# Decay exponents in gated cross attention: the key side carried by the same product as the peaks

## The chip, the cores and the metric

The kernel runs on one core of a Trainium2 chip. The metric is the device time of one execution in microseconds; three executions of the kernel before took 3082.6, 3076.7 and 3079.26 us, with a median of 3079.26 us.

## What is computed

Two layers act on `x` of 32 sequences with 512 tokens and 512 features. The first is a gated cross attention of 8 heads of 64 in the manner of an mLSTM: its queries are the normalized rows of `x`, its keys and values are the raw `ctx` rows, and each score is multiplied by a decay factor. The second is a feed-forward layer of 8 experts, in which each expert takes the 2048 tokens with its highest probabilities. The change lies in the first layer, whose core is:

```python
log_f = log_sigmoid(fg)                       # gates: a linear map of q and ctx, 8 heads
cs = cumsum(log_f, axis=-1)
log_D = where(tril, cs[..., :, None] - cs[..., None, :], -inf) + ig[..., None, :]
max_log_D = max(log_D, axis=-1, keepdims=True)
D = exp(log_D - max_log_D)
C = (q @ k.T / sqrt(64)) * D
h = (C / (maximum(abs(C.sum(-1)), exp(-max_log_D)) + 1e-6)) @ v
x = x + tanh(g) * (normalize_per_head(h) * out_w)
...
x = x + tanh(g2) * experts(layernorm(x))
```

## The kernel before, in words

**Stages.** An attention stage goes through the 32 sequences one by one and takes the first third of the time; it leaves the new `x`, its normalized rows and the expert probabilities in memory. The rest is the experts, which the change doesn't touch.

**Attention as a pipeline.** Each of the five engines has a hand-written program with a loop `for i in range(NB + 2)`; one pass is called a round. In round i an engine works on several sequences at once: `b1 = i - 1` has its gates computed and its keys and queries turned, `b2 = i - 2` has its scores weighted and its values summed, `b3 = i - 3` gets its heads normalized and added to `x`, `b4` and `b5` have the new rows normalized. Each engine runs its instructions strictly in the written order and waits on semaphores; nothing reorders them. A sequence is cut into four tiles of 128 tokens: within a tile the scores are computed in full, and between tiles a state `S` is carried.

**Decay exponents.** Within a tile the exponent of a key s and a query t is rise[s] minus a peak over the keys up to t. `gate_runs` on VectorE writes `rise` (L1052), 32 rows for each of the four tiles (`QD`), the first 16 of which hold the 8 heads twice: once for the rounded part and once for the remainder that the rounding leaves, since the matrix product takes rounded numbers (fp32r). GpSimd's `split_climb` (L383) makes the two parts, `climb_low` and `climb`. `gate_peaks` on VectorE (L1057) writes `peaks` in the same manner. TensorE's `decays(b, p)` (L741) gathers the exponents of a pair of heads p in the tile `EX`: first four products lay the causal mask (L749), then two products of 64x512 add the key side, with `climb` as weights and `pick` as the columns that choose heads (L754), then four products of 64x256 subtract the peaks, with `sel` as the constant weights that choose a head (L760). The two halves of the array's rows work beside each other. ScalarE takes the exponential of `EX` into `C` (L457), and VectorE multiplies it with the scores `QK` (L1017).

**Order around the change.** TensorE's round holds `decays(b2, 1)`, `decays(b2, 2)`, `decays(b2, 3)` and at its end `decays(b1, 0)`. Ahead of `decays(b2, 3)` stands `shift_gates(b1)` (L706), which moves the input gates to the rows of the forget gates for `rise`. Which PSUM bank a transpose, a state or a gate product fills is laid down in the list of `iteration_fills`, whose last number is a bank: 0 and 1 are `T`, 2 and 3 are the two halves of `QK`; for a half of `QK` a fill waits until VectorE has weighted the scores in it. GpSimd's round is: `centred_values(b1)` (`vc`), wait for VectorE's reciprocal roots (`nn`, L960), weigh the heads of b3 (L233, four tiles), `split_climb(b1)`, weigh the columns (L240, four tiles), add tile 0 to `x` (L246), the weighted values `uv` of b1 (L379), add tiles 1 to 3, which ends with the signal `x2`. VectorE waits for `x2` of a round in the next one, ahead of the row statistics of b4 (`st`, L903), and everything behind them on VectorE waits with it, among it the roots that lead to `nn`. SyncE issues all loads and stores of the stage on one queue.

## Time and profile before

| | before |
|---|---|
| median of three runs | 3079.26 us |
| the profiled execution | 3074.24 us |
| its span, first to last instruction | 3072.5 us |
| TensorE busy over the span | 2964.4 us (96%) |
| VectorE, ScalarE, GpSimd busy | 1832.6, 1138.2, 1057.8 us |
| mean granted clock of TensorE | 0.986 |

All rows are from that one profiled execution. A time stands in microseconds from the span's start; a row that joins several instructions of one line gives the start of the first and the time to the end of the last. An idle time in brackets names what ended it. Rows of 100 to 1000 us belong to the attention stage.

### The profile page before, as it was taken

How to read it: one execution, taken by the hardware profiler on the slowest of the kernel's cores; microseconds unless marked ns; L12 is line 12 of the kernel's file. 1: busy time of each engine (PE TensorE's matmuls, PEld its weight loads, DVE VectorE, ACT ScalarE, POOL GpSimd, SP SyncE). 2: the span in 40 equal slices, each digit the busy share in tenths (PEclk: the TensorE clock that was granted, in tenths of full speed). 3: DMA queues.
4: the chain of work that ended last, by engine and by line, in shares of the span. 5: the costliest groups of instructions: out<-in, count | busy, mean ns of one | idle time of the engine just before them, and what ended most of it. 6: DMA issues, size and time to landing. Idle time of an engine off the chain costs nothing.

```text
span 3072.5 us, 60746 instructions
## 1 busy us (share of the span) xinstructions
PE 2964.4 (96%) x24708; PEld 2398.2 (78%) x24708; DVE 1832.6 (60%) x5124; ACT 1138.2 (37%) x2025; POOL 1057.8 (34%) x1028
## 2 busy tenths in 40 slices
PE   6999999999997599999999999999999999999998
PEld 5888888888886477777777777787787777778886
DVE  6999998999998645354454444445435444444322
ACT  5778787877886311121121121122112112112110
POOL 4767687777766211111112111121112111121111
PEclk9999999999998799999999999999999999999999
DMA  3243434434342422231242131232123214222121
GB/s 129 84 166 113 167 135 144 158 121 167 130 149 104 137 42 35 37 99 31 44 100 47 37 79 34 37 95 62 31 37 88 45 31 110 37 49 58 35 37 23
DMA packets 140062, 250.68 MB, mean 82 GB/s; under 512 B 31457, under 2 KB 31457, under 8 KB 139785
## 3 DMA queue, kind: packets, MB, share of 16 engines
q1 hardware_dynamic: 105784, 170.80, 16.5%
q0 software_dynamic: 28672, 67.65, 12.5%
q10 hardware_dynamic: 5328, 8.36, 0.9%
q8 instruction: 196, 3.21, 0.4%
q14 instruction: 82, 0.66, 0.1%
HBM read 137.23 MB, written 101.19 MB: 78 GB/s over the span
## 4 chain that ended last, share of the span: by engine, by line
PE 63%; DMA 2%; DVE 1%; issue 0%; ACT 0%; POOL 0%; ACTq 0%; DVEq 0%; POOLq 0%
PE DN L1710 31%; PE UP L1684 29%; PE TT L1657 2%; DMA w_raw<-in_L_ffn_W_down 2%; DVE c_hit L1380 0%; DVE down_lo L1246 0%; PE c_bank L1373 0%; ACT z L1629 0%; PE c_bank L1357 0%; DVE c_hit L1401 0%; DVE c_within L1396 0%; ACT down_hi L1240 0%; POOL out_x L1604 0%; DVE mid_lo L1742 0%; DVE c_gained L1433 0%
## 5 line engine op out<-in xcount | busy, mean ns | idle before, releaser
L1604 POOL DMA_INDIRECT out_x<-y,slots x128 | 202.0, 1578 | 1640.5 <-DVE y L1764 1640.5
L1710 PE MATMUL DN<-down_hi,mid_hi 128*128 128x512 f32 x1408 | 579.2, 411 | 0.0
L1629 ACT ACTIVATE z<-UP,bup 128x512 f32<-128x512 f32 (+1 forms) x352 | 240.8, 686 | 853.8 <-PE UP L1684 836.9
L1684 PE MATMUL UP<-xT_hi,up_hi 128*128 128x512 f32 (+1 forms) x1408 | 553.1, 393 | 1.9 <-DVE xT_lo L1721 0.9
L1684 PE MATMUL UP<-xT_hi,up_lo 128*128 128x512 f32 (+1 forms) x1408 | 554.8, 394 | 0.0
L1684 PE MATMUL UP<-xT_lo,up_hi 128*128 128x512 f32 (+1 forms) x1408 | 551.3, 392 | 0.0
L1710 PE MATMUL DN<-down_hi,mid_lo 128*128 128x512 f32 x1280 | 505.1, 395 | 0.0
L1710 PE MATMUL DN<-down_lo,mid_hi 128*128 128x512 f32 x1280 | 504.9, 394 | 0.0
L1740 DVE CAST mid_hi<-z 128x512 fp32r<-128x512 f32 (+1 forms) x352 | 151.1, 429 | 484.3 <-ACT z L1629 484.3
L1613 ACT ACTIVATE xT_hi<-TT 128x512 fp32r<-128x512 f32 x126 | 75.1, 597 | 702.9 <-PE TT L1657 682.9
L1684 PEld LDWEIGHTS UP<-xT_hi,up_hi 128*128 128x128 f32 (+1 forms) x1408 | 259.8, 185 | 68.5 <-ACT z L1629 4.5
L1684 PEld LDWEIGHTS UP<-xT_lo,up_hi 128*128 128x128 f32 (+1 forms) x1408 | 259.3, 184 | 66.7
L1684 PEld LDWEIGHTS UP<-xT_hi,up_lo 128*128 128x128 f32 (+1 forms) x1408 | 259.6, 184 | 65.3
L1710 PEld LDWEIGHTS DN<-down_hi,mid_hi 128*128 128x128 f32 x1408 | 265.6, 189 | 51.9
L1710 PEld LDWEIGHTS DN<-down_hi,mid_lo 128*128 128x128 f32 x1280 | 240.0, 187 | 58.7
L1762 DVE TENSOR_TENSOR y<-DN,bdn 128x512 f32<-128x512 f32 x128 | 88.5, 692 | 330.5 <-PE DN L1710 326.1
L1710 PEld LDWEIGHTS DN<-down_lo,mid_hi 128*128 128x128 f32 x1280 | 241.1, 188 | 46.0
L1742 DVE TENSOR_TENSOR mid_lo<-z,mid_hi 128x512 fp32r<-128x512 f32 (+1 forms) x352 | 244.3, 694 | 12.1
L233 POOL TENSOR_TENSOR nsb<-nsb,rr 128x512 f32<-128x512 f32 x125 | 127.0, 1048 | 225.2 <-DVE nn L960 225.2
L1017 DVE SCALAR_TENSOR_TENSOR C<-QK,C 128x512 f32<-128x512 f32 x256 | 164.7, 685 | 8.5 <-PE QK L738 6.5
L903 DVE BATCH_NORM_STATS2 st<-xs 128x6 f32<-128x512 f32 x248 | 152.9, 679 | 14.4 <-DMA xs<-in_x 14.0
L738 PE MATMUL QK<-qT,kT 64*128 64x128 f32 x2048 | 147.3, 283 | 14.7 <-DVE S L1035 13.6
(263 smaller groups left out, 5005.3 us busy)
## 6 DMA issues: line engine op xcount, KB each, us to landing
xs<-in_x SPq DMA_DIRECT2D x32, 1024.0 KB, 8.3
kraw<-in_ctx SPq DMA_DIRECT2D x32, 1024.0 KB, 5.7
out_x<-xs SPq DMA_DIRECT2D x32, 1024.0 KB, 12.7
rows_scratch<-xfb SPq DMA_DIRECT2D x32, 1024.0 KB, 10.8
w_raw<-in_L_ffn_W_down SPq DMA_DIRECT2D x40, 512.0 KB, 4.4
w_raw<-in_L_ffn_W_up SPq DMA_DIRECT2D x16, 682.5 KB, 4.1
mid_hi<-mid_hi ACTq DMA_DIRECT2D x32, 86.0 KB
mid_lo<-mid_hi ACTq DMA_DIRECT2D x32, 84.0 KB
```

Of the source, the lines that this page charges most:

```text
L233: ins = eng.tensor_tensor(n, n, spread(scale[:, j, :], 2, DH), ALU.mult)
L738: mm = pe.matmul(QK[:, par, jj], kT[r, b % 2, p, jj], qT[r, b % 2, p, jj], start=True, stop=True)
L903: dve.bn_stats(st[:, which, j, :], src[:, j, :]).then_inc(s["dchain"], 1)
L1017: dve.scalar_tensor_tensor(out=c, in0=QK[:, par, :], scalar=DH ** -0.5, in1=c, op0=ALU.mult, op1=ALU.mult)\
L1604: pool.indirect_dma_start(out_rows, bass.IndirectOffsetOnAxis(ap=slots[:, m:m + 1], axis=0), y[:, t, :], None, compute_op=ALU.add).then_in ...
L1613: act.activation(xT[0][:, c, :], turned(n, c)[:, :], ACT.Copy).then_inc(s["thi"], 1)
L1629: act.activation(z[0:r, k % 2, :], UP[k % 3][0:r, :], ACT.Silu, bias=bup[0:r, e // 2, f:f + 1]).then_inc(s["z"], 1)
L1684: mm = pe.matmul(UP[k % 3][0:r, :], weights.up[wa][:, c, f * P:f * P + r], xT[xa][:, c, :], start=first, stop=(c == CH - 1 and wa == 1))
L1710: mm = pe.matmul(DN[m % 2][:, :], lhs, rhs, start=first, stop=(f == FCH - 1 and lhs is parts[-1][0]))
L1740: dve.tensor_copy(mid[0][0:r, f, :], z[0:r, k % 2, :]).then_inc(s["hi"], 1)
L1742: dve.tensor_tensor(mid[1][0:r, f, :], z[0:r, k % 2, :], mid[0][0:r, f, :].bitcast(FP32), ALU.subtract)\
L1762: dve.tensor_tensor(y[:, t, :], DN[m % 2][:, :], bdn[:, e % 2, :], ALU.add).then_inc(s["yp"], 1)
```

## The change

The `climb` and `pick` products leave `decays`. Instead the four products that subtract the peaks carry the key side too. Their weights are no longer the constant `sel` but a tile `climbs`, which holds for each head the parts of `rise` in rows that were empty before, masked to that head by `ofhead`, and -1 in the rows of the peaks; against the `rise` rows stand ones in `peaks`, laid once among the constants. For this the 16 rows of `rise` of each tile must move by 16 partitions: SyncE copies them to a tile `lift` with four small copies for each sequence (`lift_rise`), and `split_climb` works on `lift`. `spread_climb` on GpSimd writes `climbs`, first for the heads of pair 0, later for the other six. `climbs` has one buffer where `climb` had two. The weighted values of b1 now come ahead of all four row sums, and the first column product ahead of `split_climb`. `shift` gets bank 2 in place of 1, and `scores(b2, 3)` waits for it to be taken.

```diff
-        sel = sb("sel", [P, HEADS, P], FP32R); selP = sb("selP", [P, HEADS, DH], FP32R)
+        climbs = sb("climbs", [P, HEADS, P], FP32R); ofhead = sb("ofhead", [P, HEADS]); selP = sb("selP", [P, HEADS, DH], FP32R)
...
-        climb = sb("climb", [P, 2, P], FP32R); climb_low = sb("climb_low", [P, P], FP32R)
-        pick = sb("pick", [P, PAIRS, 2, 2], FP32R)
+        climb = sb("climb", [P, P], FP32R); climb_low = sb("climb_low", [P, P], FP32R)
+        lift = sb("lift", [P, P]); lift_lows = sb("lift_lows", [P, TILES])
...
-                    ("qw", b2, 2, "dve", 1), ("scores", b2, 2, None, None), ("shift", b1, 0, "dve", 1), ("qw", b2, 3, "dve", 1),
+                    ("qw", b2, 2, "dve", 1), ("scores", b2, 2, None, None), ("shift", b1, 0, "dve", 2), ("qw", b2, 3, "dve", 1), ("scores", b2, 3, None, None),
...
+                def lift_rise(b):
+
+                    wait_taken(sp, "shift", b, 0)
+                    if b:
+                        sp.wait_ge(s["rp"], b)
+                    for j in range(TILES):
+                        at = QD * j
+                        sp.dma_start(lift[at + 2 * HEADS:at + QD, :], rise[at:at + 2 * HEADS, :]).then_inc(s["lifted"], 16)
...
                     store_probabilities(i - 7)
+                    if live(i - 1):
+                        lift_rise(i - 1)
...
-                        if row % QD < 2 * HEADS:
-                            step(pool.affine_select(out=heads[:, :], in_=heads[:, :], compare_op=ALU.not_equal, fill=1.0,
+                        for one in (heads, ofhead) if row % QD < 2 * HEADS else (ofhead,):
+                            step(pool.affine_select(out=one[:, :], in_=one[:, :], compare_op=ALU.not_equal, fill=1.0,
...
-                    step(pool.tensor_scalar(sel[:, :, :], spread(heads[:, :], 2, P), -1.0, None, ALU.mult))
...
+                    for n in range(2):
+                        step(pool.tensor_copy(peaks[:, n, :], C[:, 5, :]))
...
-                    wait_taken(pool, "shift", b, 0)
-                    if b >= 2:
-                        pool.wait_ge(s["ee"], 2 * PAIRS * (b - 1))
-                    step(pool.tensor_scalar(climb_low[:, :], rise[:, :], lows[:, 0:1], None, ALU.mult))
-                    pool.tensor_tensor(climb[:, b % 2, :], rise[:, :], climb_low[:, :].bitcast(FP32), ALU.subtract).then_inc(s["rp"], 1)
+                    pool.wait_ge(s["lifted"], 16 * TILES * (b + 1))
+                    step(pool.tensor_scalar(climb_low[:, :], lift[:, :], lift_lows[:, 0:1], None, ALU.mult))
+                    pool.tensor_tensor(climb[:, :], lift[:, :], climb_low[:, :].bitcast(FP32), ALU.subtract).then_inc(s["rp"], 1)
                     pool.wait_ge(s["rp"], b + 1)
+                    if b:
+                        pool.wait_ge(s["ee"], 2 * PAIRS * b)
+                    spread_climb(b, 0, 2)
+
+                def spread_climb(b, first, end):
+
+                    heads_of = climbs[:, first:end, :]
+                    pool.tensor_tensor(heads_of, spread(climb[:, :].bitcast(FP32), 1, end - first), spread(ofhead[:, first:end], 2, P), ALU.mult)\
+                        .then_inc(s["cl"], 1)
+                    pool.wait_ge(s["cl"], 2 * b + (1 if first == 0 else 2))
...
-                    if p == 0:
-                        pe.wait_ge(s["rp"], b + 1)
-                    for a, r in ((0, top), (1, end)):
-                        ones_of = pick[r, p, :, :].rearrange("k a j -> k (a j)")
-                        pe.matmul(EX[:, a, :], climb[r, b % 2, :], spread(ones_of, 2, P), start=False, stop=False, skip_group_check=True)
+                    if p < 2:
+                        pe.wait_ge(s["cl"], 2 * b + p + 1)
...
-                            mm = pe.matmul(EX[:, a, par * 2 * P:(par + 1) * 2 * P], sel[r, 2 * p + par, :], peaks[r, b % 2, half],
+                            mm = pe.matmul(EX[:, a, par * 2 * P:(par + 1) * 2 * P], climbs[r, 2 * p + par, :], peaks[r, b % 2, half],
...
                     if b >= 1:
-                        dve.wait_ge(s["rp"], b)
+                        dve.wait_ge(s["lifted"], 16 * TILES * b)
...
-                        rows = slice(QD * j, QD * j + QD)
+                        rows = slice(QD * j, QD * j + 2 * HEADS)
```

How this stands on the engines is shown at three places; each row is a line of the kernel, an operation, its tiles and the count of equal neighbours. The first is GpSimd's round from the heads of b3 (`nsb`) to the row sums, before and then after:

```order
L233 TENSOR_TENSOR nsb<-nsb,rr 128x8x64 x4
L388 TENSOR_SCALAR climb_low<-rise,lows 128x128
L389 TENSOR_TENSOR climb<-rise,climb_low 128x128
L240 TENSOR_TENSOR nsb<-nsb,Wo 128x8x64 x4
L246 TENSOR_TENSOR xs<-xs,nsb 128x512
L379 TENSOR_TENSOR uv<-vc,tm 128x520 x3
L246 TENSOR_TENSOR xs<-xs,nsb 128x512 x3
```

```order
L233 TENSOR_TENSOR nsb<-nsb,rr 128x8x64 x4
L240 TENSOR_TENSOR nsb<-nsb,Wo 128x8x64
L404 TENSOR_SCALAR climb_low<-lift,lift_lows 128x128
L405 TENSOR_TENSOR climb<-lift,climb_low 128x128
L414 TENSOR_TENSOR climbs<-climb,ofhead 128x256
L240 TENSOR_TENSOR nsb<-nsb,Wo 128x8x64 x3
L397 TENSOR_TENSOR uv<-vc,tm 128x520 x3
L414 TENSOR_TENSOR climbs<-climb,ofhead 128x768
L246 TENSOR_TENSOR xs<-xs,nsb 128x512 x4
```

Two products with `climbs` have come in ahead of the row sums, one column product has moved ahead of `climb_low`, and the weighted values stand ahead of all row sums. The second place is TensorE from `shift` to the scores of pair 3:

```order
L706 MATMUL T<-gsum,shift 128x128
L749 MATMUL EX<-maskneg,identb 64x512
L749 MATMUL EX<-maskswap,identb 64x512 x2
L749 MATMUL EX<-maskneg,identb 64x512
L754 MATMUL EX<-pick,climb 128x512 x2
L760 MATMUL EX<-peaks,sel 128x256 x4
L768 MATMUL T<-inner,selP 128x384
L713 MATMUL T<-ends,later 128x8
L714 MATMUL T<-unseen,ident 128x4
L738 MATMUL QK<-qT,kT 128x128 x8
```

```order
L734 MATMUL QK<-gsum,shift 128x128
L777 MATMUL EX<-maskneg,identb 64x512
L777 MATMUL EX<-maskswap,identb 64x512 x2
L777 MATMUL EX<-maskneg,identb 64x512
L785 MATMUL EX<-peaks,climbs 128x256 x4
L793 MATMUL T<-inner,selP 128x384
L741 MATMUL T<-ends,later 128x8
L742 MATMUL T<-unseen,ident 128x4
L766 MATMUL QK<-qT,kT 128x128 x8
```

The pair of products with `climb` is gone, and `shift` fills a half of `QK`. The third place is SyncE's round:

```order
L290 DMA kraw<-in_ctx 128x4x512 [waits a_vc,a_tfull]
L294 DMA xs<-in_x 128x4x512 [waits a_xf2,a_xst0]
L259 DMA rows_scratch<-xfb 128x4x512 [waits a_xf2]
L254 DMA out_x<-xs 128x4x512 [waits a_x2]
L264 DMA rows_scratch<-sm_all 128x4x8 [waits a_smx]
L284 DMA lift<-rise 16x128 [waits a_rp,a_td]
L284 DMA lift<-rise 16x128 x3
```

The five large transfers of a round stand as before, and the four copies to `lift` have come in behind them.

## Rows read from the trace of the kernel before

**Rows 1.** Stretches, `rise` to `rise`: length, busy by engine (instructions), PEclk, DMA share, GB/s

```profile
85.11:113.20 28.09, 26.59 (x444) 22.16 (x442) 26.45 (x72) 19.10 (x38) 20.05 (x21) 1.00 0.22 77
...
469.59:498.74 29.15, 28.79 (x491) 24.55 (x487) 27.20 (x78) 23.61 (x47) 21.82 (x23) 1.00 0.44 147
529.05:559.65 30.60, 30.37 (x491) 25.84 (x487) 27.30 (x78) 23.31 (x47) 20.49 (x22) 0.94 0.41 140
...
sum 830.48, PE 811.47 PEld 689.52 DVE 763.37 ACT 659.61 POOL 611.51; mean PE 28.98 PEld 24.63 DVE 27.26 ACT 23.56 POOL 21.84
```

**Rows 2.** Waits from 100 to 1000 us: total, times, longest

```profile
PE QK L738 <- DVE S L1035: 12.9, 26, 0.9
DVE st L903 <- DMA xs<-in_x: 10.1, 13, 2.2
DVE qw L1026 <- PE T L768: 9.5, 24, 1.0
DVE rise L1052 <- PE T L706: 5.6, 13, 1.4
```

**Rows 3.** TensorE in order of time: start, length, line, operation, count, idle before

```profile
485.42 1.16 PE L738 MATMUL QK<-qT,kT 64*128 64x128 f32 x16 [0.36 <-DVE S L1035]
...
498.15 0.49 PE L706 MATMUL T<-gsum,shift 128*128 128x128 f32 x2
...
498.91 0.48 PE L754 MATMUL EX<-pick,climb 64*128 64x512 f32 x2
499.23 0.40 PE L760 MATMUL EX<-peaks,sel 64*128 64x256 f32 x4
...
504.62 0.48 PE L754 MATMUL EX<-pick,climb 64*128 64x512 f32 x2
...
512.69 0.48 PE L754 MATMUL EX<-pick,climb 64*128 64x512 f32 x2
```

**Rows 4.** VectorE in order of time, the same stretch

```profile
487.83 2.46 DVE L903 BATCH_NORM_STATS2 st<-xs 128x6 f32<-128x512 f32 x4
...
496.59 0.17 DVE L960 SCALAR_TENSOR_TENSOR nn<-mv,rr 128x8 f32<-128x8 f32 x1
...
498.74 0.29 DVE L1052 TENSOR_TENSOR rise<-T,cs 128x128 f32<-128x128 f32 x1 [0.30 <-PE T L706]
```

**Rows 5.** GpSimd in order of time, from the heads to the row sums

```profile
496.90 4.05 POOL L233 TENSOR_TENSOR nsb<-nsb,rr 128x512 f32<-128x512 f32 x4 [6.74 <-DVE nn L960]
501.05 0.61 POOL L388 TENSOR_SCALAR climb_low<-rise,lows 128x128 fp32r<-128x128 f32 x1
501.74 0.46 POOL L389 TENSOR_TENSOR climb<-rise,climb_low 128x128 fp32r<-128x128 f32 x1
502.28 4.61 POOL L240 TENSOR_TENSOR nsb<-nsb,Wo 128x512 f32<-128x512 f32 x4
...
508.14 3.08 POOL L379 TENSOR_TENSOR uv<-vc,tm 128x520 f32<-128x520 f32 x3
511.29 3.46 POOL L246 TENSOR_TENSOR xs<-xs,nsb 128x512 f32<-128x512 f32 x3
```

**Rows 6.** Store of `sm_all` on SyncE: shortest, median, longest issue (ns) and landing

```profile
L264 SPq DMA_DIRECT2D rows_scratch<-sm_all x32: 360/1904/2438, 191.1 to 1007.6; - x32
...
DMA to landing us min/median/max: 1.8/12.5/13.3
```

**Rows 7.** Transfers of the whole run: line's tiles, KB, us from issue to landing

```profile
tanh_g<-in_g_ffn ACTq DMA_DIRECT2D x1, 0.5 KB, 2.6
```

**Rows 8.** The stretch from 497 to 498 us, columns as in the first group

```profile
497.00:498.00 1.00, 1.00 (x26) 0.93 (x22) 0.96 (x2) 0.94 (x5) 1.00 (x2) 1.00 0.09 26
```

**Rows 9.** Prologue in order of time, GpSimd's constants

```profile
9.21 0.61 POOL L318 CAST selP<-C 128x512 fp32r<-128x512 f32 x1
9.91 2.79 POOL L319 TENSOR_SCALAR sel<-C 128x1024 fp32r<-128x1024 f32 x1
```

**Rows 10.** TensorE's first product with `peaks`

```profile
33.71 0.80 PE L760 MATMUL EX<-peaks,sel 64*128 64x256 f32 x4 [2.13 <-DVE peaks L1071]
```

More of the change, by code:

```diff
@@ L303, in _ @@
                 step = Chain(pool, s["pchain"])
+                step(pool.memset(lift[:, :], -1.0))
                 for n in range(2):
@@ L325, in constants @@
-                    step(pool.tensor_tensor(lows[:, 0:2], lows[:, 0:2], lows[:, 2:4], ALU.add))
-                    step(pool.tensor_tensor(lows[:, 0:1], lows[:, 0:1], lows[:, 1:2], ALU.add))
+                    for rows, first in ((lows, HEADS), (lift_lows, 3 * HEADS)):
+                        step(pool.memset(rows[:, :], 1.0))
+                        step(pool.affine_select(out=rows[:, :], in_=rows[:, :], compare_op=ALU.is_ge, fill=0.0,
+                                                base=-first, pattern=[[-QD, TILES]], channel_multiplier=1))
+                        step(pool.affine_select(out=rows[:, :], in_=rows[:, :], compare_op=ALU.is_ge, fill=0.0,
+                                                base=first + HEADS - 1, pattern=[[QD, TILES]], channel_multiplier=-1))
+                        step(pool.tensor_tensor(rows[:, 0:2], rows[:, 0:2], rows[:, 2:4], ALU.add))
+                        step(pool.tensor_tensor(rows[:, 0:1], rows[:, 0:1], rows[:, 1:2], ALU.add))
@@ new lines, in constants @@
+                    ones_of = C[:, 5, :].rearrange("p (j t) -> p j t", j=TILES)
+                    step(pool.memset(ones_of, 1.0))
+                    step(pool.affine_select(out=ones_of, in_=ones_of, compare_op=ALU.is_ge, fill=0.0,
+                                            base=-2 * HEADS, pattern=[[-QD, TILES], [0, P]], channel_multiplier=1))
+                    step(pool.affine_select(out=ones_of, in_=ones_of, compare_op=ALU.is_ge, fill=0.0,
+                                            base=QD - 1, pattern=[[QD, TILES], [0, P]], channel_multiplier=-1))
@@ L334, in constants @@
                                             base=QD - 1, pattern=[[QD, TILES]], channel_multiplier=-1))
-                    step(pool.tensor_tensor(wt[:, 0:2], own[:, 0:2], own[:, 2:4], ALU.add))
-                    step(pool.tensor_tensor(pick[:, :, :, :].rearrange("k p a j -> k (p a) j"), spread(heads[:, :], 2, 2),
-                                            spread(wt[:, 0:2], 1, HEADS), ALU.mult))
                     step(pool.memset(unseen[:, :], 0.0))
@@ L400, in _ @@
                         weigh_heads(step, pool, b3, slice(0, TILES))
+                    if live(b3):
+                        weigh_columns(step, pool, b3, slice(0, 1))
                     if live(b1):
@@ L403, in _ @@
                     if live(b3):
-                        weigh_columns(step, pool, b3, slice(0, TILES))
+                        weigh_columns(step, pool, b3, slice(1, TILES))
+                    if live(b1):
+                        weigh_v(b1)
+                        spread_climb(b1, 2, HEADS)
+                    if live(b3):
                         for j in range(TILES):
-                            if j == 1 and live(b1):
-                                weigh_v(b1)
                             ins = add_rows(pool, b3, j)
@@ L885, in _ @@
                 ins.then_inc(s["clear"], 1)
-                for t in (gW[:, :, :], peaks[:, :, :].bitcast(FP32), inner[:, :, :].bitcast(FP32)):
+                for t in (gW[:, :, :], inner[:, :, :].bitcast(FP32)):
                     step(dve.memset(t, 0.0))
```

10 lines of the change are left out of this document (2 added, 8 removed).

## The prediction
> **What bounds the kernel now.** I read first the table of stretches, cut at the decay chain's `rise` of each sequence, because the diff touches the attention stage alone. A sequence takes 29.15 us where nothing disturbs it, and 28 sequences take 830.48 us, 29.66 each [rows 1]. TensorE is busy for 28.79 of the 29.15 us, VectorE for 27.20, GpSimd for 21.82 [rows 1]. This looks like a TensorE bound, but the list of waits says that it is nearly two bounds: TensorE waits for VectorE's `S` (12.9 us in 26 waits) and VectorE waits for TensorE's `qw` fill (9.5 us, 24) and for its `shift` product (5.6 us, 13) [rows 2]. So the two hand the lead to each other: TensorE leads from the scores of pair 1 (it waited 0.36 us there) to `shift`, VectorE from `rise` (it waited 0.30 us) to `S` [rows 3, 4].
>
> There is a third ring, and the change puts its new work into it. VectorE ends `nn` at 496.59 + 0.17 = 496.76; GpSimd starts on the heads at 496.90 and ends the row sums (`x2`) at 511.29 + 3.46 = 514.75 [rows 4, 5]. VectorE needs `x2` for the row statistics of the next round, which stand at 487.83 in this one, so at 516.98 a period later; from there to its next `nn` it works 496.76 - 487.83 = 8.93 us without a wait of note [rows 4]. The ring is thus 0.14 + 17.85 + 8.93, with about 0.1 us for the signal of `x2` (an estimate between the handovers seen in these rows, 0.04 to 0.15): 27.02 us. It fits into 29.15 with 2.1 us to spare. GpSimd is idle long enough, but its idle time stands ahead of the heads, where it waits for `nn`, not inside this run.
>
> **TensorE: two products fewer for each pair.** The 64x512 products with `climb` start at 498.91 and those with `peaks` at 499.23 [rows 3]; the two run beside each other on the two halves of the array, so a pair gives up 0.32 us, a sequence 4 x 0.32 = 1.28 us, 32 sequences 41 us. The product that now carries both sides keeps its shape (four of 64x256), so it costs nothing more. If TensorE alone set the time, 41 us would come back. It doesn't: in the path that alternates, TensorE leads over one pair only (pair 2) and VectorE's wait for `qw` ends earlier by the 0.32 us of another (pair 3). VectorE's wait of 0.30 us for `shift` goes, and 0.32 of the 0.40 us (9.5 in 24 [rows 2]) for `qw`; then it is full: 29.15 - 0.62 = 28.5 us for a sequence is the floor of these two engines. The rest of the 1.28 us becomes waiting of TensorE.
>
> **GpSimd: the heads are spread.** New are a product of 128x256 (pair 0) ahead of most of the column weights and one of 128x768 behind the weighted values, both ahead of the row sums, so both inside the third ring. The trace has no such instruction. The nearest are products of two inputs, one of them repeated: 128x520 at 3.08 us for three [rows 5], 1.03 us each and 1.06 with the 0.03 us by which neighbours overlap, and the `climb` difference of 128x128 at 0.46 us [rows 5]. A line through 0.46 and 1.06 gives 0.27 us + 1.53 ns a column: 0.66 and 1.43 us, 2.09 us together. From below, a cast of 128x512 takes 0.61 us with one input [rows 9], two such sizes 1.2 us; from above, the old `sel`, a 128x1024 product with a constant, took 2.79 us [rows 9], with a second start about 3.0. I take 2.09, whose rows have the operation and the operands. The extra steps cost their handovers: one more between the first and the other three column weights (0.10 us), one behind each spread (0.08 us each, as between 501.05 + 0.61 and 501.74 [rows 5]), and the overlap of 0.03 us of a row sum with the weighted values: 0.28 us. The run becomes 17.85 + 2.09 + 0.28 = 20.22 us and the ring 0.14 + 20.22 + 0.10 + 8.93 = **29.4 us**. That is above the two-engine floor of 28.5 and above the undisturbed 29.15.
>
> The page "GPSIMD Engine Reference" of the Trainium skill, section "Elementwise — side-by-side cycle accounting", speaks against the move: a product of two tensors costs GpSimd some 2.2 ns a column (4497 ns for 2048 columns), about twice VectorE's price. The rows here show 2.0 with a repeated operand; by the page's figure the spreads would be 2.25 us (an estimate) and the ring 29.55.
>
> **Spreading pair 0 first, weighted values earlier.** Counted from `nn`, GpSimd now ends pair 0 at 7.4 us (0.14 + 4.05 heads + 0.10 + 1.19 first column, a quarter of 4.61 with its overlap + 0.09 + 0.61 + 0.08 + 0.46 + 0.08 + 0.66). TensorE reached that product 504.62 - 498.15 = 6.47 us behind the start of `shift` [rows 3] and now 0.32 us less; with `shift` about 0.7 us behind `nn`, since it now lies in a score bank and must wait until VectorE has weighted those scores, that is 6.9 us. So it waits some 0.5 us, which its 1.28 us pay. Its next product of this kind comes 512.69 - 504.62 = 8.07 us later [rows 3], less 0.32: 15.2; heads 2 to 7 are ready at 15.6. Another 0.4 us of waiting, also covered. The weighted values begin at 11.0 us behind `nn`, 0.3 earlier than the 508.14 of before [rows 5], and TensorE's use of them keeps its distance. Behind the row sums stand SyncE's store of `x` and GpSimd's next values; the store leaves 2.3 us later, and the slot that it empties is loaded again only a round after that.
>
> **SyncE: four small copies.** `rise` ends some 2.0 us behind `nn` (the 0.30 us wait for `shift` is gone). SyncE wakes and issues four copies of 8 KB, at 0.36 us or a little more each [rows 6], the last at about 3.3. From issue to landing the trace has 1.8 us at the least for a store on this queue when nothing stands ahead of it [rows 6], and 2.6 us for a small load [rows 7]. The copies land between 5.1 and 5.9; GpSimd comes for them at 5.5. So they cost between 0 and 0.4 us in the ring, and I take 0, for the store is on the same queue. The queue is empty then: the engines' share falls to 0.09 at 497 us, a microsecond ahead of `rise` [rows 8]. If the cover failed, each 0.1 us would cost 2.8 us of the time. Queued behind the waiting SyncE are only the loads of the next round, issued 14 us later.
>
> **What disturbs now and then.** The mean lies 0.51 us above 29.15. Part is the wait for `xs` (10.1 us in 13 [rows 2]); VectorE comes for it 0.9 us later after the change, so most of this goes. Part is two sequences in which the granted clock averaged 0.94 of full speed (one of them 30.60 us [rows 1]) and a few stalls of TensorE; about 0.7 us of each is now covered by the ring. I leave 2.5 us in all.
>
> **Ends.** GpSimd's constants grow: sixteen more selections, `lift_lows`, `ones_of` and two copies of 128x512 into `peaks` (0.61 us each by the cast [rows 9]), less the 2.79 us of `sel`: about 6 us, an estimate. VectorE's first gates hardly feel it, but pair 0 of the first sequence waited for `peaks` until 33.71 [rows 10] and will wait for GpSimd until about 35: 1.2 us. The two first rounds, without row sums, win 0.7 us each; the fourth goes from 28.09 us [rows 1] to 29.4, a loss of 1.3.
>
> **Sum.** 27 full rounds at 29.4 in place of 29.66: -7.3 us; a last short round -0.6; disturbances +2.5; ends 1.2 - 1.4 + 1.3 = +1.1. Together -4 us. The profiled execution took 3074.24 us, 1.7 more than its span of 3072.5 and 5.0 less than the median of the three runs, 3079.26; the difference is carried to the median: **3075 us**.
>
> **Rivals.** (a) *The third ring doesn't decide*: the spreads cost near their lower end, 1.2 us. Then the ring is 28.5, level with the two engines' floor; 27 x (29.66 - 28.6) = 28 us, less the disturbances and ends: 3053. For it: GpSimd's price a column is read from shapes at most 520 wide. Against: the cast is an operation with one input, and GpSimd's products of two run at one price here, four of them in 4.05 to 4.61 us [rows 5]. (b) *Slower, by the landing of the copies*: issue at 0.45 us each and landing at 2.6 us put `lift` at 6.1 behind `nn`, 0.6 us into the ring: 30.0 us, +17 us, 3092. It decides from 5.5 us on, and only there. For it: the small load took 2.6 us; against: the idle queue's 1.8. The Trainium skill's page "DMA: Bandwidth & Descriptors", section "Anatomy of one DMA — SWDGE (gpsimd) path", gives about 2.0 us fixed, which would put the landing at 5.3 (an estimate), inside the cover. (c) *Slower, by the spreads at `sel`'s price*, 3.0 us: ring 30.3, 3100. (d) *The change doesn't save what it says*: the `climb` products were hidden beside weight loads and TensorE's 28.79 us stay near 28.5; with the two new waits of 0.9 us a sequence takes 29.5 and the time is 3081. Against: the next product's start moves with them in all four pairs.
>
> **Chances.** Forecast 0.52 (3066 to 3085), (a) 0.17, (b) 0.18, (c) 0.06, (d) 0.07. About 0.2%, 6 us, is what a measurement of this kernel can tell from no change. Of the forecast's share a third falls under 3073, so faster has 0.17 + 0.17 = 0.34; slower 0.15 + 0.06 + 0.03 + 0.02 = 0.26; the same 0.40. The range of 8 in 10 takes in the cheap spreads and the late copies: 3053 to 3094.
>
> **What would show it.** In the profile of the changed kernel: VectorE waits for GpSimd's `xs` at the second row statistics, about 1 us in each round (step "ring"); TensorE's idle time grows by about 1.5 us a sequence, mostly at the products with `climbs`; the two spreads take 0.66 and 1.43 us; GpSimd waits for `lift` less than 0.2 us; `rise` to `rise` is 29.4 us and steadier. If VectorE never waits for `x2`, (a) is right; if GpSimd's wait ahead of `climb_low` is over 0.4 us, (b).

## The result, and the profile after

Slower: 3144.27 us (median of 4 runs, 3135.57 to 3147.56) against 3078.5 us for the kernel before on the same chip; the ratio is 1.0212 with a 95% interval of 1.0197 to 1.0227, some 66 us. The prediction said 3075 us and a range up to 3094. The profiled execution took 3144.76 us, its span 3143.0 us, the mean granted clock was 0.973 of full speed (0.986 before).

Stretches of the kernel after from `rise` to `rise`, as in [rows 1] (length; busy PE, PEld, DVE, ACT, POOL; PEclk, DMA share, GB/s). The sum is over the 27 rounds from 117 to 976 us:

```profile
532.43:562.97 30.54, 28.35 (x481) 23.79 (x483) 28.45 (x77) 23.59 (x47) 23.91 (x25) 1.00 0.41 141
562.97:594.36 31.39, 28.35 (x481) 23.79 (x483) 29.31 (x78) 23.74 (x47) 23.89 (x25) 1.00 0.41 138
...
626.40:659.31 32.91, 31.18 (x481) 26.28 (x483) 29.31 (x77) 23.44 (x47) 23.89 (x25) 0.90 0.38 131
...
sum 858.97, PE 802.67 PEld 674.31 DVE 772.94 ACT 636.26 POOL 645.29; mean PE 29.73 PEld 24.97 DVE 28.63 ACT 23.57 POOL 23.90
```

A mean round is 31.81 us in place of 29.66 [rows 1]. From the first `rise` to the last the kernel takes 61.7 us more (976.2 against 914.5), out of 70.5 us by which the spans of the two profiles differ; nearly all of the rest lies behind the last `rise`, and its cause is open. There are three kinds of round: undisturbed ones of 30.5 us (the first row), ones at full clock that are longer all the same (the second), and ones in which TensorE's granted clock averages 0.95 or less, mostly 0.90 or 0.95 (the third). The prediction had 29.4 for all.

GpSimd in the undisturbed round, in order of time (start, length, line, operation, count, idle before), answering to [rows 5]:

```profile
531.01 4.05 POOL L233 TENSOR_TENSOR nsb<-nsb,rr 128x512 f32<-128x512 f32 x4 [5.75 <-DVE nn L985]
...
537.69 0.61 POOL L414 TENSOR_TENSOR climbs<-climb,ofhead 128x256 fp32r<-128x256 f32 x1
...
545.12 1.47 POOL L414 TENSOR_TENSOR climbs<-climb,ofhead 128x768 fp32r<-128x768 f32 x1
546.67 4.61 POOL L246 TENSOR_TENSOR xs<-xs,nsb 128x512 f32<-128x512 f32 x4
...
551.75 4.05 POOL L387 TENSOR_TENSOR vc<-kraw,hs 128x512 f32<-128x512 f32 x4
```

VectorE in the same round, answering to [rows 4]:

```profile
551.32 2.47 DVE L928 BATCH_NORM_STATS2 st<-xs 128x6 f32<-128x512 f32 x4 [0.59 <-POOL xs L246]
...
554.24 0.60 DVE L969 TENSOR_TENSOR top<-nsb,tm 128x32 f32<-128x32 f32 x1
554.88 0.97 DVE L970 SCALAR_TENSOR_TENSOR top<-nsb,top 128x32 f32<-128x32 f32 x1
555.88 0.18 DVE L971 TENSOR_SCALAR top<-top 128x32 f32<-128x32 f32 x1
...
561.24 0.17 DVE L985 SCALAR_TENSOR_TENSOR nn<-mv,rr 128x8 f32<-128x8 f32 x1
```

Here the ring of the prediction can be read off. GpSimd works from 531.01 to 551.28, VectorE takes `x2` 0.04 us later (it had waited 0.59 us for it) and ends `nn` at 561.41: 0.14 + 20.27 + 0.04 + 10.09 = 30.54 us, the length of the round. It closes as foretold, and in 27 of 28 rounds: there VectorE takes `x2` within 0.1 us of its end. But VectorE's part is 10.09 us and not 8.93. The two instructions on `top` (L969, L970) take 0.60 and 0.97 us, and 0.21 each in rounds where GpSimd is idle beside them: 1.15 us. They stand beside GpSimd's `vc`, which follows the row sums at once. In the kernel before, `vc` (GpSimd, until 519.27) was over when VectorE came to them:

```profile
515.22 4.05 POOL L369 TENSOR_TENSOR vc<-kraw,hs 128x512 f32<-128x512 f32 x4
```

```profile
519.90 0.21 DVE L944 TENSOR_TENSOR top<-nsb,tm 128x32 f32<-128x32 f32 x1
520.15 0.21 DVE L945 SCALAR_TENSOR_TENSOR top<-nsb,top 128x32 f32<-128x32 f32 x1
```

Below, "company" means GpSimd at work beside such small instructions of VectorE.

Waits from 100 to 1000 us (total, times, longest), answering to [rows 2]:

```profile
POOL climb_low L404 <- DMA lift<-rise: 24.2, 17, 1.9
...
PE QK L734 <- DVE C L1042: 20.6, 16, 2.1
PE EX L785 <- POOL climbs L414: 13.6, 25, 1.3
...
DVE st L928 <- POOL xs L246: 12.6, 17, 1.0
```

GpSimd waits for the copies in 17 rounds, 1.4 us in the mean; a wait for `xs` from memory no longer stands in the list. The copies themselves, SyncE's line L284 (issue in ns at the least, median, most; landing in us):

```profile
L284 SPq DMA_DIRECT2D lift<-rise x112: 512/589/1578, 117.5 to 978.3; - x112
...
DMA to landing us min/median/max: 1.6/1.7/3.5
```

### The profile page after: what moved, and what is told of

It reads as the page before. It is cut to its first block, busy times and chain, and to the rows that moved or that the text cites. A ratio compares the mean times of both kernels' runs of the same rounds, so it can differ in the third digit from the quotient of the medians.

```text
span 3143.0 us, 60592 instructions
## 1 busy us (share of the span) xinstructions
PE 2982.9 (95%) x24452; PEld 2404.1 (76%) x24452; DVE 1867.8 (59%) x5123; ACT 1137.7 (36%) x2025; POOL 1129.9 (36%) x1117
## 4 chain that ended last, share of the span: by engine, by line
PE 61%; DMA 2%; DVE 2%; issue 0%; ACT 0%; POOL 0%; ACTq 0%; DVEq 0%; POOLq 0%
PE DN L1735 31%; PE UP L1709 28%; DMA w_raw<-in_L_ffn_W_down 2%; PE TT L1682 2%; DVE c_hit L1405 0%; DVE down_lo L1271 0%; PE c_bank L1398 0%; ACT z L1654 0%; PE c_bank L1382 0%; DVE c_hit L1426 0%; DVE mid_lo L1767 0%; DVE c_within L1421 0%; ACT down_hi L1265 0%; POOL out_x L1629 0%; DVE mid_hi L1765 0%
## 5 line engine op out<-in xcount | busy, mean ns | idle before, releaser
L766 PE MATMUL QK<-qT,kT 64*128 64x128 f32 x2048 | 161.1, 302 | 8.8 <-DVE S L1060 8.0
L928 DVE BATCH_NORM_STATS2 st<-xs 128x6 f32<-128x512 f32 x248 | 153.0, 679 | 18.4 <-POOL xs L246 13.6
```

Of the source, the lines that this page charges most:

```text
L766: mm = pe.matmul(QK[:, par, jj], kT[r, b % 2, p, jj], qT[r, b % 2, p, jj], start=True, stop=True)
L928: dve.bn_stats(st[:, which, j, :], src[:, j, :]).then_inc(s["dchain"], 1)
```

## The experiments

Ratios are to the kernel before on the same chip, with their 95% interval. "Mean round" is over the same 27 rounds of the profile.

### The spreads alone, in the kernel before

**e3**: GpSimd makes both spreads into a tile that nobody reads; `sel` is kept once for each head, to make room.

```diff
+        step(pool.tensor_tensor(unread[:, 0:n, :], spread(climb[:, b % 2, :].bitcast(FP32), 1, n), spread(ofhead[:, 0:n], 2, P), ALU.mult))
```

> The kernel before with GpSimd's new work alone: two products of 128x256 and 128x768 into a tile that nobody reads, at the places where the change spreads the heads, and nothing else of the change (no copies by SyncE, climb products kept; to make room in memory the constant sel is held once for each head and repeated by its address pattern). Theory A: the ring becomes 0.14 + 20.1 + 0.05 + 10.1 = 30.4 us, so a round takes 30.4 in place of 29.7 and the time is 3095 to 3110; VectorE's two long instructions go from 0.21 to 0.6 and 0.97 us. If the ring doesn't decide, the time stays within 6 us of before.

Measured: 3100.39 us, 1.007 (1.0048 to 1.0092), rounds of 30.4, mean 30.50. With TensorE's work as before, 2.1 us on GpSimd cost 22 us. The number is the one expected, but by luck, for the ring stays open. In the round shown, GpSimd ends `x2` at 495.87 + 3.46 = 499.33 and VectorE comes for it at 499.85 without having waited; this slack of some 0.5 us stands in nearly every round. What grew is VectorE's own path. `sm_all` lasts 1.24 us (over 0.9 in 25 of 28 rounds) and the second `top` 0.90, beside GpSimd's `vc` here too; the kernel before had 0.19 and 0.21. That is 1.7 us more for a round that became 1.2 longer; VectorE's waits for TensorE took up the rest.

```profile
480.65:511.03 30.38, 28.88 (x483) 24.26 (x483) 28.88 (x78) 23.71 (x47) 23.88 (x25) 1.00 0.42 141
```

```profile
495.87 3.46 POOL L246 TENSOR_TENSOR xs<-xs,nsb 128x512 f32<-128x512 f32 x3
```

```profile
488.73 1.24 DVE L936 TENSOR_TENSOR sm_all<-ex,sx 128x32 f32<-128x32 f32 x1
...
499.85 2.46 DVE L910 BATCH_NORM_STATS2 st<-xs 128x6 f32<-128x512 f32 x4
...
503.01 0.90 DVE L952 SCALAR_TENSOR_TENSOR top<-nsb,top 128x32 f32<-128x32 f32 x1
```

`sm_all` in the kernel before:

```profile
506.93 0.19 DVE L929 TENSOR_TENSOR sm_all<-ex,sx 128x32 f32<-128x32 f32 x1
```

**e10**: e3 without the climb's two products for each pair (the exponents lack the climb).

```diff
-                        pe.matmul(EX[:, a, :], climb[r, b % 2, :], spread(ones_of, 2, P), start=False, stop=False, skip_group_check=True)
```

> The kernel before with GpSimd's two spreads (as in e3, whose rounds were 30.4 us at clock 1.00 and which took 3100 us), and now also without the climb's two products in each pair (so the exponents lack the climb): TensorE's load is that of the changed kernel, with no copies, no new wait of TensorE, and shift in its old bank. Theory clock: a lighter TensorE under a ring of 30.4 us waits about 2 us in each round, is granted the lower clock in some of them as the changed kernel without copies is (mean round 31.4 us, clock 0.974), and the kernel takes 3115 to 3130 us, slower by some 20 us although it does less. Rival ring alone: the rounds stay at 30.4 us whatever TensorE does, 3095 to 3103 us, and the clock dips of the changed kernel are due to its new waits.

Measured: 3106.85 us, 1.0103 (1.0081 to 1.0126); 21 of 27 rounds at clock 1.00 (26 in e3), mean round 30.75. Less work for TensorE won nothing and brought five more rounds at a lower clock; by time the two intervals overlap, so a loss is likely and not shown.

### VectorE's small instructions beside GpSimd

**e4, e1**: the variances (L969 to L974) ahead of the wait for `x2`, in the kernel before (e4) and after (e1).

```diff
+                    if live(b3):
+                        head_variances(b3)
                     if live(b4):
                         wait_x2(dve, b4)
...
-                    if live(b3):
-                        head_variances(b3)
```

> The kernel before with the same edit as the first of these runs (head variances ahead of the wait for x2). In the kernel before that wait is over long before, so theory A expects no more than 6 us either way, 3072 to 3085; if it moves by more, the order on VectorE matters in itself and the first run doesn't show the ring alone.

> The changed kernel with one edit on VectorE: the five small instructions of the head variances stand ahead of the wait for x2 instead of behind the row statistics. Theory A (the ring nn, GpSimd's run, x2, VectorE's run back to nn decides every round): the run back shrinks from 10.1 us to about 7.5, since 2.6 us of it (1.2 us of work, 1.2 to 1.4 us of two of its instructions standing while GpSimd works) leave it; a round falls from 31.8 us to 29.0 to 29.6, the time from 3144 to 3065 to 3090, and the granted clock in the attention stage rises, as TensorE waits less. Theory B (the low granted clock is a cause of its own that comes with fewer TensorE columns): the rounds stay at 31 us or more and the time at 3125 or more. The two long instructions should still be long (0.6 and 0.9 us) if GpSimd's row sums stand beside them, short (0.21) otherwise.

Measured: e4 3123.72 us, 1.0154 (1.0128 to 1.0179), steady rounds of 30.81; e1 3154.78 us, 1.025 (1.0229 to 1.0271). e4 missed its expectation and e1 its theory A; e1's time lies in the range of theory B, but the rows show another cause. In e4 VectorE now comes to the variances while `vc` runs (GpSimd's row first):

```profile
504.46 4.05 POOL L369 TENSOR_TENSOR vc<-kraw,hs 128x512 f32<-128x512 f32 x4
```

```profile
506.05 0.50 DVE L944 TENSOR_TENSOR top<-nsb,tm 128x32 f32<-128x32 f32 x1
506.59 0.97 DVE L945 SCALAR_TENSOR_TENSOR top<-nsb,top 128x32 f32<-128x32 f32 x1
507.59 0.96 DVE L946 TENSOR_SCALAR top<-top 128x32 f32<-128x32 f32 x1
```

In e1 the first three escape and the last two meet it; `vc` starts at 556.00:

```profile
555.69 0.21 DVE L970 SCALAR_TENSOR_TENSOR top<-nsb,top 128x32 f32<-128x32 f32 x1
555.93 0.18 DVE L971 TENSOR_SCALAR top<-top 128x32 f32<-128x32 f32 x1
556.15 0.94 DVE L972 SCALAR_TENSOR_TENSOR top<-top 128x32 f32<-128x32 f32 x1
557.12 0.97 DVE L974 SCALAR_TENSOR_TENSOR vv<-ssq,top 128x32 f32<-128x32 f32 x1
```

The same instructions last 0.2 us alone and up to 0.97 in these rows beside GpSimd, about one of GpSimd's pieces (4.05 us for four). In the attention stage of the kernels before and after, e1, e3, e4 and e10, 369 executions of the variances' instructions and of `sm_all` lasted over 0.4 us, and every one ended 0.03 to 0.05 us behind the end of an instruction of GpSimd: VectorE's instruction stands until that one has ended. This costs time even where no ring closes: VectorE comes for `x2` 5.0 us after it is ready in e4, 2.6 in e1 and 0.5 in e3 (medians). The Trainium skill's page "SBUF — State Buffer", section "SBUF: two separate sides", says that VectorE's instructions with two SBUF inputs and GpSimd's shut each other out of a shared pair of ports for a whole instruction. The rows agree for the two-input ones. The one-input L946 took 0.96 us too; it is a `TENSOR_SCALAR`, which the section "Who interferes with whom" of the same page of the Trainium skill says can run in a two-port mode that shares those ports, and no run here tells which mode it ran in.

**e7**: in the kernel after, the variances behind the new sequence's row statistics, when `vc` is over.

```diff
                         step(row_moments(xs[:, i % XBUF, :, :], 0))
+                    if live(b3):
+                        head_variances(b3)
                     row_variances(i)
```

> The changed kernel with the five small instructions of the heads' variances behind the row statistics of the new sequence instead of ahead of them, so that GpSimd's product vc, which begins once nn is used, has begun and mostly ended before they run. Theory ring with company: VectorE's run from x2 to nn falls from 10.1 towards 8.9 us where top is back at 0.21 us each, so rounds lose up to 1.1 us: 3105 to 3120 us. If top is still 0.6 and 0.97 us (GpSimd's rows products beside it): 3140 to 3150 us. Rival clock and late copies alone set the length: 3135 to 3150 us with top short.

Measured: 3151.37 us, 1.0231 (1.02 to 1.0263). `top` was back at 0.21 us, and nothing was won: VectorE now waited for the new `x`.

```profile
DVE st L928 <- DMA xs<-in_x: 29.9, 25, 2.7
```

**e11**: in the kernel after, ScalarE spreads heads 2 to 7 at the end of its round.

```diff
+                    for h in range(2, HEADS):
+                        ins = act.activation(climbs[:, h, :], climb[:, :].bitcast(FP32), ACT.Identity, scale=ofhead[:, h:h + 1])
```

> The changed kernel with the spread of heads 2 to 7 taken from GpSimd: ScalarE makes them at the end of its round, six instructions of 128x128 (its others of that shape take 0.28 to 0.39 us, so 1.8 us). GpSimd's stretch from nn to x2 falls by 1.47 to 18.9 us; if the ring closes at all it does so at about 28 us with top back at 0.21 us. Theory ring first: rounds are then set by TensorE and VectorE as before, 28.9 to 29.8 us, 3055 to 3090 us, and the clock dips get rarer since TensorE is busy for a larger part of a shorter round. Rival: copies and clock hold it, rounds of 30 us and more with clock under 0.97: 3095 to 3125 us.

Measured: 3136.53 us, 1.0183 (1.0134 to 1.0232), mean round 31.79, although GpSimd's ring no longer closed (VectorE comes for `x2` 1.3 us or more after it is ready). One round of 33.06 us, all at clock 1.00, was followed. Its rows on SyncE's queue, and VectorE's wait:

```profile
670.11 0.38 SPq L290 DMA_DIRECT2D kraw<-in_ctx  x1
671.05 0.38 SPq L294 DMA_DIRECT2D xs<-in_x  x1
```

```profile
681.02 2.47 DVE L938 BATCH_NORM_STATS2 st<-xs 128x6 f32<-128x512 f32 x4 [2.23 <-DMA xs<-in_x]
```

`rise` of that round stood at 654.06. The load of `kraw` goes out 16.05 us later, once the chunk states have freed its buffer; `x` follows 0.94 us behind it on the same queue, lands 9.97 us later, the statistics reach `nn` in 4.54 and the next `rise` comes in another 1.56: 33.06 us. That is a second ring, over the loads, which lies just behind the first.

**e16, e12, e13, e15**: the load of `x` ahead of that of `kraw`; alone in the kernel after (e16), with e7 (e12), with e11 (e13), and alone in the kernel before (e15).

```diff
+                    if XBUF <= i < NB:
+                        sp.wait_ge(s_xst[i % XBUF], 16 * (i // XBUF))
+                        sp.wait_ge(s["xf2"], i - XBUF + 1)
+                        sp.dma_start(xs[:, i % XBUF, :, :], x_v[i]).then_inc(s_xl[i % XBUF], 16)
                     if VBUF <= i < NB:
                         wait_filled(sp, "st", i - VBUF, TILES - 2)
```

> The changed kernel with the load of x ahead of kraw's and nothing else: the control for e12 and e13. Theory two rings, the x2 ring in front: VectorE waits for no x in the changed kernel, the ring with company is 30.46 us with or without the edit, and the kernel stays at 3135 to 3150 us, mean round 31.5 to 31.9. Rival (the loads' order alone made e12 and e13 faster): 3095 to 3115 us.

> The changed kernel with the variances behind the new sequence's row statistics (as e7, 3151 us, mean round 32.0) and with the load of x ahead of kraw's load on SyncE's queue, so that its megabyte moves first. Theory second ring: x lands some 2.5 us earlier (5.6 us after its issue, as kraw does now, in place of 8.1), VectorE's waits for it (29.9 us in 25) go, the x2 ring without company is 29.3 us, and the kernel drops to 3100 to 3125 us with rounds at clock 1.00 of 29.3 to 29.6. Rival (neither ring decides; TensorE's waits and clock do): the waits for x go but the mean round stays at 31.5 us or more, 3130 to 3150 us.

> The changed kernel with heads 2 to 7 spread by ScalarE (as e11, 3137 us, mean round 31.8) and with the load of x ahead of kraw's. One round of e11 was followed through the trace: x issued 17.0 us after rise, landed 27.0, the next rise at 33.06, all of it at clock 1.00. Theory second ring: with x landing 2.5 us earlier that round is 30.5 us or less; mean round 29.5 to 30.5, 3075 to 3105 us. Rival: another wait takes its place (TensorE for qT or climbs, GpSimd for the copies), mean round 31 us or more, 3120 to 3140 us.

> The kernel before with the load of x ahead of kraw's, nothing else. VectorE waits for x there 10.1 us in 13 waits between 100 and 1000 us. If such a wait moves rise one for one, some 10 us per 28 rounds go: 3066 to 3072 us. If VectorE catches up by the next meeting with TensorE: 3076 to 3082 us, no difference.

Measured: e16 3140.99 us, 1.0202 (1.0183 to 1.0222); e12 3101.29 us, 1.0074 (1.005 to 1.0098); e13 3100.62 us, 1.0083 (1.006 to 1.0107); e15 3069.52 us, 0.9977 (0.9965 to 0.9989). The order of the loads alone does nothing for the kernel after, nor does taking away the company alone (e7); both together win 1.4%. Two rings of nearly one length hide each other. An undisturbed round of e12 and its `top`:

```profile
452.14:481.50 29.36, 28.28 (x481) 23.77 (x483) 27.27 (x78) 23.46 (x47) 23.91 (x25) 1.00 0.43 147
```

```profile
477.15 0.21 DVE L969 TENSOR_TENSOR top<-nsb,tm 128x32 f32<-128x32 f32 x1
477.40 0.22 DVE L970 SCALAR_TENSOR_TENSOR top<-nsb,top 128x32 f32<-128x32 f32 x1
```

29.36 us is the ring that the prediction worked out. In e15 24 of 28 rounds last 29.16 or 29.17 us: the second ring had disturbed the kernel before too [rows 2], and e15 is faster than that kernel by 0.2%.

### The copies into `lift`

**e5, e17**: no copies; GpSimd waits for `rise` itself and splits the unwritten tile `lift`. In the kernel after (e5) and in e12 (e17).

```diff
-                    if live(i - 1):
-                        lift_rise(i - 1)
...
-                    pool.wait_ge(s["lifted"], 16 * TILES * (b + 1))
+                    wait_taken(pool, "shift", b, 0)
```

> The changed kernel without the four copies of rise into lift: GpSimd waits for rise itself, as the kernel before did, and splits a tile lift that is never written after its start (so the exponents are those of other numbers; every product and every spread stays). Rounds of the changed kernel that nothing disturbs last 30.5 us, the mean one 31.8 us. Theory late copies: the copies hold GpSimd up to 1.9 us, it reaches the heads' other spread and x2 later, and TensorE, which waits for these and for score banks, falls to the lower clock: without them the mean round is 30.5 to 30.8 us and the kernel takes 3100 to 3112 us. Rival shift's bank: the long rounds come from the product of shift, which waits for a bank that VectorE's weighted scores leave late; the copies are a symptom: 3130 to 3145 us still.

> e12 (variances last, x first; 3101 us, mean round 30.24) without the copies of rise into lift (GpSimd waits for rise and splits the unwritten tile lift, so the exponents are those of other numbers). Theory late copies: in e12 the rounds without a late copy last 29.4 us and the others 30.3 to 30.9; without copies nearly all last 29.3 to 29.5, and the kernel takes 3070 to 3082 us, level with the kernel before although GpSimd still makes both spreads. Rival: other waits of TensorE (climbs, shift's bank) keep the mean round at 30 us or more, 3090 to 3105 us.

Measured: e5 3123.48 us, 1.0141 (1.0109 to 1.0172), some 11 us above what the theory of the copies expected, with 15 of 27 rounds still at a lower clock; e17 3082.09 us, 1.0004 (0.9992 to 1.0016). The copies cost 0.7% in the one pair and 0.7% in the other. Two rounds of e5 in a row, 30.46 us at full clock and 32.57 at 0.90:

```profile
461.98:492.44 30.46, 28.33 (x481) 23.78 (x483) 28.38 (x77) 23.59 (x47) 23.88 (x25) 1.00 0.40 141
492.44:525.01 32.57, 31.27 (x481) 26.38 (x483) 28.56 (x78) 23.41 (x47) 23.87 (x25) 0.90 0.40 132
```

A round of e17, its ring on GpSimd and on VectorE:

```profile
407.51:436.84 29.33, 28.27 (x481) 23.79 (x483) 27.25 (x77) 23.48 (x47) 23.90 (x25) 1.00 0.43 146
```

```profile
406.09 4.05 POOL L233 TENSOR_TENSOR nsb<-nsb,rr 128x512 f32<-128x512 f32 x4 [4.60 <-DVE nn L974]
...
421.69 4.61 POOL L246 TENSOR_TENSOR xs<-xs,nsb 128x512 f32<-128x512 f32 x4
```

```profile
426.33 2.48 DVE L917 BATCH_NORM_STATS2 st<-xs 128x6 f32<-128x512 f32 x4 [0.57 <-POOL xs L246]
...
435.11 0.17 DVE L974 SCALAR_TENSOR_TENSOR nn<-mv,rr 128x8 f32<-128x8 f32 x1
```

0.14 + 20.21 + 0.03 + 8.95 = 29.33 us, where the prediction had 0.14 + 20.22 + 0.10 + 8.93.

### TensorE's load, the bank of `shift`, GpSimd's order

**e2, e9**: two products with zeros for each pair, the shape of those that the change removed, in the kernel after (e2) and in e5 (e9).

```diff
+                    for a, r in ((0, top), (1, end)):
+                        pe.matmul(EX[:, a, :], climbs[r, 2 * p, :], spread(none[r, :], 2, P), start=False, stop=False, skip_group_check=True)
```

> The changed kernel with TensorE's work put back: in every pair two products of 64x512 with columns of zeros, as the removed climb products had them (they add zero to the exponents). Theory A: the ring of 30.5 us stays, so the time can't fall under about 3100; TensorE waits less between its products, so if waiting is what lets the granted clock fall, the clock goes back to 0.98 or more and the time falls to 3100 to 3115. Theory B (fewer columns as such): the same clock and the same gain. Theory C (the clock has nothing to do with it and TensorE's length counts): the time rises by up to 41 us, to 3150 to 3185.

> The changed kernel without the copies into lift (GpSimd waits for rise and splits the unwritten tile lift, so the exponents are those of other numbers) and with two products of 64 rows by 512 columns of zeros put back into each pair, the shape of the climb's two products that the change takes out. TensorE has the load of the kernel before again. Without the copies the rounds at a granted clock of 1.00 lasted 30.46 us, those at 0.95 31.1 to 31.5, those at 0.90 32.5. Theory clock: what is left above 30.46 comes from TensorE's waits, after which it is granted the lower clock; with its old load it waits less, the clock is 1.00 nearly throughout, the mean round 30.5 to 30.7 us: 3098 to 3108 us. Rival (the waits make the long rounds, and the clock only goes with them): TensorE's longer work costs what it costs, mean round 31.3 us or more, 3120 to 3135 us.

Measured: e2 3140.66 us, 1.0205 (1.0183 to 1.0227); e9 3114.24 us, 1.0126 (1.0104 to 1.0149). In e9 22 of 27 rounds ran at clock 1.00 (mean 30.45 us) against 12 in e5 (mean 30.46), and the mean round fell from 31.39 to 30.83. So with more work TensorE kept the higher clock in more rounds (mean clock of the four executions 0.979 to 0.982, against 0.973 to 0.974 in e5), and where the ring decides the work cost nothing; by time the two intervals overlap. In e2 the clock of the profiled execution rose to 0.981 and the time stayed, while the copies still came late (22.1 us in 18 waits): the clock alone was not the cause.

**e6, e8**: `shift` back in bank 1, in the kernel after (e6) and in e5 (e8).

```diff
-  ... ("shift", b1, 0, "dve", 2), ("qw", b2, 3, "dve", 1), ("scores", b2, 3, None, None),
+  ... ("shift", b1, 0, "dve", 1), ("qw", b2, 3, "dve", 1),
```

> The changed kernel with the product of shift back in bank 1, where the kernel before has it, and without the entry on which the fourth pair's scores wait for that bank. Theory shift's bank: shift no longer waits for the weighted scores of pair 2 (20.6 us in 16 waits between 100 and 1000 us of the trace, plus 7.8 us put down to issue), TensorE stays at the higher clock, mean round 30.5 to 30.9 us, 3100 to 3115 us. Rival late copies: the waits only move to the next thing that is late; the rounds stay at 31.5 us or more, 3130 to 3145 us.

> Both edits together: no copies into lift and shift in bank 1. What is left of the change is TensorE's 32 products fewer in a sequence's pairs, GpSimd's two spreads and its order. Theory that copies and bank are all that separates the changed kernel from the kernel before with GpSimd's spreads (3100 us, rounds of 30.4 us): 3095 to 3105 us, rounds 30.4 to 30.6 us with clock 1.00. If the order on GpSimd (uv ahead of row sums) or TensorE's shorter work with its waits holds something of it: 3110 to 3130 us.

Measured: e6 3135.92 us, 1.0181 (1.015 to 1.0212); e8 3131.19 us, 1.0165 (1.0133 to 1.0197), no better than e5. In e6 TensorE's 28 us of waits at `shift` became 23 us at the product with `inner` behind it (L793), which waits for `rise`. The bank is not the cause.

**e14**: the first row sum ahead of the weighted values again.

```diff
+                    if live(b3):
+                        ins = add_rows(pool, b3, 0)
                     if live(b1):
                         weigh_v(b1)
```

> The changed kernel with one thing put back: GpSimd takes the first row sum ahead of the weighted values uv again (so the heads' second spread comes 1.15 us later too). In the changed kernel GpSimd waits for uv's factors 15.4 us in 12 rounds of 28, up to 2.5 us, and the ring pays for each. Theory order: those waits go under the row sum, 10 to 17 us over the run: 3125 to 3136 us. Rival: TensorE waits longer for heads 2 to 7 (13.6 us in 25 waits now, up to 1.1 us more in each round), falls to the lower clock more often, and nothing or less than nothing is won: 3140 to 3160 us.

Measured: 3139.78 us, 1.0197 (1.0172 to 1.0221): between its two expectations and within the uncertainty of the kernel after. GpSimd's waits for the factors of `uv` fell from 15.4 to 1.4 us, TensorE's for `climbs` rose from 13.6 to 24.7 us. The new order of GpSimd neither costs nor wins what can be measured.

## Why the prediction was wrong

The loss divides into two causes that add up. Company and loads (e7's and e16's edits together): 1.0212 to 1.0074 with the copies, 1.0141 to 1.0004 without, 42 us both times. Copies: 1.0212 to 1.0141 and 1.0074 to 1.0004, 22 us both times. Each difference carries some 8 to 11 us of uncertainty, from the intervals in quadrature. Without either, the changed kernel stands level with the one before. Part of that is the order of the loads, which helps the kernel before too: with it in both, 1.0004 stands against 0.9977 (e17, e15), so some 8 us of the loss remain, with 5 us of uncertainty.

- **TensorE's saving: oversized, and of no weight.** Its busy time in an undisturbed round fell from 28.79 us [rows 1] to 28.35, 0.44 us and not 1.28; e9 against e5 gives 0.79 for the same shape of product. What it saved became waiting, as the prediction said.
- **The third ring: right.** Spreads 0.61 and 1.47 us (0.66 and 1.43 foretold); heads of pair 0 ready 7.43 us behind `nn` (7.4), the others at 15.72 (15.6); GpSimd's run 20.27 us (20.22); VectorE waits for `x2`. By the figure of the Trainium skill's page "GPSIMD Engine Reference", section "Elementwise — side-by-side cycle accounting" (4497 ns for an addition of two tensors of 2048 columns), the spreads would have been 2.25 us (an estimate); the rows gave 2.08.
- **VectorE's run back of 8.93 us: the step that failed first.** It was read from a round in which GpSimd was idle beside the variances [rows 4] and carried over to a ring that closes, where GpSimd turns from the row sums straight to `vc` beside them. It became 10.09 us, the ring 30.54 in place of 29.4: some 31 us over 27 rounds. e3, e4 and e1 show that such company lengthens VectorE's path with the ring open too; the prediction had no term for it.
- **The copies: the second step that failed.** "I take 0" rested on 0.36 us for an issue; it was 0.59, 2.41 us for the four, so the last copy went out 3.7 us behind `nn` and not 3.3. Landing in 1.7 us it just meets GpSimd at 5.5, with no cover left, and in 17 of 28 rounds it landed later. This is rival (b): the point from which it decides was right, its 17 us were measured as 22. The 2.0 us of the Trainium skill's page "DMA: Bandwidth & Descriptors", section "Anatomy of one DMA — SWDGE (gpsimd) path", stand there for DMAs that GpSimd issues; these copies are SyncE's.
- **The covered disturbances: wrong.** The ring was to cover TensorE's stalls. But TensorE's spare time under a longer ring went with rounds at a lower clock, which no term priced: in e5 12 rounds at 1.00 average 30.46 us, 7 at 0.90 average 32.72. The 2.5 us left for all disturbances came out as 27 x (31.81 - 30.54) = 34 us, the late copies among them.
- **The wait for `xs`: half right.** It went, as foretold; that the loads form a ring of their own close behind was not seen, and it is what made e7 and e11 look like failures of the theory.
- Rivals (a) and (c) fell by the spreads' measured length. Rival (d) was near in its premise, as TensorE's busy time fell to 28.35 us and it foretold 28.5, but the ring set the time.

What stays open: how much of the 42 us is company and how much the loads, which win only together; how much of company's cost goes through the ring; how much of each cause passes through the lower clock, and what makes it fall in one round and not in the next.

## What to carry to other kernels

When a change moves or lengthens one engine's work, every time that the sum takes from the trace has to be read again for who now works beside it: the duration of a small VectorE instruction belongs to the company it had in the trace, and this holds whether or not a ring closes (e3). Look for the next ring of nearly the same length before judging a repair, since two rings that tie need two edits at once. A transfer that lands just as its reader comes has no cover, and its worst landing counts, not its median.

## What the runs showed of the hardware

**A copy behind a piece of program.** The late copies did not wait for data traffic: the DMA share was at most 0.16 in any microsecond while those of the round at 626 us moved. In each of the 28 rounds of the kernel after from 117 to 976 us, the instruction queue q8 moved a packet of 16 KB in the 6 us behind `rise`. In the 17 rounds in which GpSimd waited over 0.5 us, the first such packet began 2.0 to 3.2 us behind `rise`, while the copies were in flight; in the 11 others 3.8 us or more, as the copies landed (3.9) or later. Its line in 0.4 us of a late round (from 629.20; `rise` at 626.40) and of one in time (from 536.83; `rise` at 532.43), as packets, MB and share of 16 engines:

```profile
q8 instruction: 1, 0.02, 22.7%
```

```profile
q8 instruction: 1, 0.02, 14.5%
```

The last copy of that late round took 3.5 us and not 1.7. This rests on times that agree, in 28 rounds; no run changed the packets.

**The lower clock.** In the kernel after the granted clock fell to 0.50, the level of 1.2 GHz, from about 500.7 to 507.5 us, behind an idle time of TensorE of 0.75 us and as a second one, of 0.27 us, began; one round later the same two did not bring it down. In single microseconds, and pair 3's scores at either level:

```profile
500.00:501.00 1.00, 0.73 (x6) 0.35 (x4) 0.93 (x4) 0.90 (x3) 1.00 (x2) 0.83 0.00 0
...
502.00:503.00 1.00, 1.00 (x10) 1.00 (x12) 0.93 (x5) 0.63 (x2) 0.92 (x2) 0.50 0.07 17
```

```profile
501.84 2.08 PE L766 MATMUL QK<-qT,kT 64*128 64x128 f32 x16
...
533.97 1.16 PE L766 MATMUL QK<-qT,kT 64*128 64x128 f32 x16
```
